# Gate and up of a ternary FFN as seven block products of half depth per four chunks and two batches, on one Trainium2 core

## What is computed

```
x = x + tanh(g_xattn) * xattn(layernorm(x), ctx, ctx, Wq, Wk, Wv, Wo, bo, g)
x = x + tanh(g_ffn)   * ffn(layernorm(x), w_gate, w_up, w_down)

def bitlinear(x, w):                       # w: 2752 x 1024, w_down: 1024 x 2752
    scale = mean(abs(w))
    q = round(clip(w / (scale + EPS), -1, 1))
    return x @ (q * scale).T
ffn(h) = bitlinear(bitlinear(h, w_gate) * bitlinear(h, w_up), w_down)
```

## Time and profile before

| | |
|---|---|
| median of 3 runs | 1417.92 us (1417.47 to 1419.09) |
| the profiled execution's own time | 1416.91 us |
| its span, first to last instruction | 1415.1 us |
| TensorE's mean granted clock | 0.985 |
| matmuls, each with a weight load | 9528 |

### The profile page before, as it was taken

The page is one execution under the profiler, slowest core; times in us unless marked ns, Lnnn a source line. Parts: engine busy times, 40 slices in busy tenths (PEclk is TensorE's granted clock), DMA queues, the critical chain, the costliest instruction groups (busy, mean ns, idle before and its releaser), DMA issues.

```text
span 1415.1 us, 23736 instructions
## 1 busy us (share of the span) xinstructions
PE 1350.5 (95%) x9528; PEld 959.8 (68%) x9528; DVE 903.9 (64%) x1369; ACT 623.3 (44%) x957; POOL 452.4 (32%) x275
## 2 busy tenths in 40 slices
PE   4786799999999999999999999999999999999999
PEld 2464487756787468774788558785787658875884
DVE  6968788877787557675675667775675747521220
ACT  4768887653545234533444333542344334320220
POOL 0159816845332413333332133323322222110000
PEclk7998999999999999999999999999999999999999
DMA  9939999976535733556433553446633644121001
GB/s 357 408 141 306 288 283 299 266 153 164 127 60 105 164 90 61 105 107 148 104 75 76 127 142 76 100 85 144 134 76 61 130 101 98 31 52 54 2 1 45
DMA packets 328429, 189.04 MB, mean 134 GB/s; under 512 B 295872, under 2 KB 296000, under 8 KB 328320
## 3 DMA queue, kind: packets, MB, share of 16 engines
q1 hardware_dynamic: 321408, 162.37, 46.7%
q10 hardware_dynamic: 6912, 25.17, 5.5%
HBM read 97.32 MB, written 16.78 MB: 81 GB/s over the span
## 4 chain that ended last, share of the span: by engine, by line
PE 82%; DVE 5%; issue 4%; DMA 3%; POOL 3%; ACT 1%; SPq 1%; ACTq 0%; POOLq 0%; DVEq 0%
PE ps L905 37%; PE ps L930 21%; PE ps L693 6%; PE ps L695 6%; PE ps L694 6%; PE ps L873 2%; DMA w_dn<-in_gate_w 1%; DMA stage_c<-in_down_tail 1%; PE ps L881 1%; PE ps L790 1%; POOL qs L1525 1%; DVE inter_buf L1150 1%; PE ps L861 1%; DVE absum L1203 1%; POOL w_dn L1495 1%
## 5 line engine op out<-in xcount | busy, mean ns | idle before, releaser
L905 PE MATMUL ps<-zT,w_gu 128*128 128x256 f16 x5504 | 626.2, 273 | 0.8 <-DVE gate L1450 0.7
L905 PEld LDWEIGHTS ps<-zT,w_gu 128*128 128x128 fp8e4 x5504 | 538.9, 98 | 81.3 <-DVE gate L1450 1.3
L930 PE MATMUL ps<-w_dn,inter_buf 128*128 128x512 fp8e4 x1376 | 304.4, 379 | 5.0 <-DVE inter_buf L1150 2.5
L930 PEld LDWEIGHTS ps<-w_dn,inter_buf 128*128 128x128 f16 x1376 | 134.6, 99 | 161.2 <-issue 6.0
L1525 POOL TENSOR_TENSOR qs<-qs,q_stat 128x1024 f32<-128x1024 f32 x64 | 126.8, 1984 | 296.6 <-DVE q_stat L1393 296.5
L942 ACT ACTIVATE gate<-ps 128x256 f32<-128x256 f32 (+1 forms) x176 | 67.1, 381 | 271.3 <-PE ps L905 268.3
L1450 DVE SCALAR_TENSOR_TENSOR gate<-ps,gate 128x256 f32<-128x256 f32 (+1 forms) x176 | 73.1, 416 | 109.2 <-ACT gate L942 108.3
L1531 POOL TENSOR_TENSOR rsv<-ssv,cst 128x4 f32<-128x4 f32 x32 | 36.7, 1147 | 240.2 <-DVE ssv L1404 240.2
L1292 DVE TENSOR_REDUCE kmx<-ps 128x1 f32<-128x1024 f32 x64 | 78.0, 1218 | 52.5 <-PE ps L695 48.9
L942 ACT ACTIVATE inter_buf<-gate 128x256 f16<-128x256 f32 (+1 forms) x176 | 72.5, 412 | 86.6 <-DVE gate L1450 86.6
L1046 ACT ACTIVATE ek<-ps,kbias,k_unit 128x1024 f32<-128x1024 f32 x56 | 67.3, 1202 | 92.8 <-DVE kbias L1301 92.8
(11 more groups left out here) (174 smaller groups left out, 1939.6 us busy)
## 6 DMA issues: line engine op xcount, KB each, us to landing
w_dn<-in_down_w SPq DMA_DIRECT2D x19, 512.0 KB, 7.0
xb<-in_x ACTq DMA_DIRECT2D x16, 512.0 KB, 4.8
x_dram<-xb SPq DMA_DIRECT2D x16, 512.0 KB, 2.9
fin<-x_dram SPq DMA_DIRECT2D x32, 256.0 KB, 3.0
out<-fin SPq DMA_DIRECT2D x32, 256.0 KB, 2.1
inter_buf<-in_up_w SPq DMA_DIRECT2D x15, 512.0 KB, 10.6
inter_buf<-in_gate_w SPq DMA_DIRECT2D x14, 512.0 KB, 9.4
w_dn<-in_gate_w SPq DMA_DIRECT2D x14, 512.0 KB, 9.2
```

The costliest lines, as they stand in the source:

```text
L905: last = nc.tensor.matmul(ps[:, j % 2, s * T:s * T + T], w_gu[:, w, k, :], zT[:, h, k, :], start=(k == 0 and h == 0), stop=(k == NC - 1 an ...
L930: mm = nc.tensor.matmul(ps[:, hf, :], lhs, w_dn[:, j, hf * 512:hf * 512 + 512], start=(u == 0), stop=(u == total - 1))
```

## The change

For groups 1 to 7, gate and up of the chunks 0 to 19 are computed in five blocks (`SU`) of four chunks. The depth of 1024 is halved (low, high), the four chunks are two pairs (half 0, half 1) and the two batches are the columns' halves. Instead of eight products of a half depth, a pair and a batch, seven are made from sums: of the weights (values -2 to 2 in fp8) and of z of the two batches. Each product (`product(g, s, q)`) is 4 weight columns x 4 depth blocks x 2 f16 halves = 32 matmuls of 128 columns in one PSUM bank. Chunk 20 and the tail keep the old way (`gu`), as does group 0.

- **Weight forms.** 35 forms (5 blocks x 7) of 128 x 2048 bytes go to a DRAM tensor `forms` in two DMAs each (`store_form`, on SP's queue) while group 0 runs. Three of seven are the quantized weights themselves; four are sums: q = 4 and q = 1 on VectorE, q = 2 and q = 5 on GpSimd, mostly in place in `w_gu` (q = 1 waits until group 0 has used the block's chunks). The first load waits for all 35.
- **Ring.** `load_form` (SP) brings a form back for each of the 245 products, 256 KB each, into a ring of 8 places; a load waits for the product 8 before it. The ring and the buffers `z16`, `zF`, `blocks` lie in the space of `w_gu` that is free by then.
- **z.** `z` moves from GpSimd to VectorE for batches 2 to 15 and works in place in `xb`, after `st_x2` has landed. When both batches' halves are made, GpSimd forms four half-width sums of z in place (`z_sum`), which are split (`zs_hi` on ScalarE, `zs_lo` on VectorE) and transposed (`turn_zs`) into `zF`. `ld_xr` of the next batch waits for this.
- **Evictions.** Products alternate between the two banks. Of seven, ScalarE copies three out (slots 0, 1, 6), VectorE adds four onto earlier ones (slots 2 to 5). Then `pair_mul` on GpSimd multiplies gate and up, `pair_hi` on ScalarE and `pair_lo` on VectorE split the result, two of each per block of 4 chunks.
- **Order.** `WHEN` is new as a whole: 3717 steps. In it 39 of the 44 `wsign` steps of gate and up stand before the first `gu` (33 before the change).

The core of the diff (the constants, the helpers of addresses and the lists of positions are left out):

```diff
-Z_SCALE = 2.0 ** 10
-I_SCALE = 2.0 ** -5
+Z_SCALE = 2.0 ** 8
+I_SCALE = 2.0 ** -6
+B_SCALE = 2.0 ** -3 / Z_SCALE
+SU = 5
+SLOTS = 7 * SU
+RING = 8
+ACT_SLOTS, DVE_SLOTS = (0, 1, 6), (2, 3, 4, 5)
+        def slot_bank(g, s, q):
+            return (first_bank(g) + 7 * s + q) % 2
...
+            def store_form(s, q):
+                if q in BASE_SLOTS:
+                    sp.wait_ge(wq_done, 2 * (4 * s + 4))
+                else:
+                    sp.wait_ge(form_made[q], s + 1)
+                wait(sp, form_stored[q], 32 * s)
+                rows = forms[(7 * s + q) * P:(7 * s + q + 1) * P, :]
+                for u in range(2):
+                    sp.dma_start(rows[:, u * 1024:u * 1024 + 1024].rearrange("p (m n) -> p m n", m=2),
+                                 form_place(s, q)[:, u, :, :]).then_inc(form_stored[q], 16)
+            def load_form(g, s, q):
+                n = SLOTS * (g - 1) + 7 * s + q
+                if n == 0:
+                    for f in range(7):
+                        sp.wait_ge(form_stored[f], 32 * SU)
+                    sp.wait_ge(gu_ready, J)
+                wait(sp, product_done, n - RING + 1)
+                x = 7 * s + q
+                sp.dma_start(ring[n % RING], forms[x * P:x * P + P, :]).then_inc(form_in[n % RING], 16)
...
+            def product(g, s, q):
+                n, m = SLOTS * (g - 1) + 7 * s + q, su_of(g, s)
+                pe.wait_ge(form_in[n % RING], 16 * (n // RING + 1))
+                if s == 0 and q in (1, 2):
+                    wait(pe, zF_in[q - 1], 16 * g)
+                if s == 0 and q < 2:
+                    wait(pe, inter32, gu_count(g, IC if q == 0 else IC - 1))
+                elif q < 2:
+                    if q == 0:
+                        wait(pe, evict_dve, 4 * m)
+                    else:
+                        wait(pe, evict_act, 3 * m)
+                elif q < 4:
+                    wait(pe, evict_act, 3 * m + q - 1)
+                else:
+                    wait(pe, evict_dve, 4 * m + q - 3)
+                form = ring[n % RING].rearrange("p (u m k i) -> p (u m) k i", u=2, m=2, k=4)
+                fresh = q not in (2, 4, 6)
+                for c in range(4):
+                    o = ps[:, slot_bank(g, s, q), c * P:c * P + P]
+                    for k in range(4):
+                        for h in range(2):
+                            last = nc.tensor.matmul(o, form[:, c, k, :], moving(q, h, k),
+                                                    start=(fresh and c == 0 and k == 0 and h == 0),
+                                                    stop=(k == 3 and h == 1), skip_group_check=True)
+                last.then_inc(product_done, 1)
...
 @@ block.scalar: ld_xr, evict @@
-                    wait(act, zT_in[i % GB], 16 * ((i - BY_PE) // GB))
+                    wait(act, zs_lo_s, 2 * (i // GB - 2) + 2 - i % 2)
+                    wait(act, z_summed, 4 * (i // GB - 1))
+            def evict(g, s, q):
+                if q not in ACT_SLOTS:
+                    return
+                wait(act, product_done, SLOTS * (g - 1) + 7 * s + q + 1)
+                wait(act, pair_lo_s, 2 * su_of(g, s) - 2 + (q == 6))
+                out = block_pair(g, s, q == 6)[:, 0 if q == 0 else 1, :]
+                copy(out, ps[:, slot_bank(g, s, q), :], B_SCALE).then_inc(evict_act, 1)
...
@@ block.vector: form, evict, pair_lo @@
+            def form(s, q):
+                if q == 4:
+                    dve.wait_ge(wq_done, 2 * (4 * s + 4))
...
+                elif q == 1:
+                    dve.wait_ge(form_made[4], s + 1)
+                    dve.wait_ge(gu_ready, 4 * s + 4)
+                    nc.vector.tensor_tensor(form_place(s, 1), form_base(s, 1, 0), form_base(s, 1, 1),
+                                            ALU.add, saturate=False).then_inc(form_made[1], 1)
+            def evict(g, s, q):
+                if q not in DVE_SLOTS:
+                    return
+                m = su_of(g, s)
+                wait(dve, product_done, SLOTS * (g - 1) + 7 * s + q + 1)
...
+                nc.vector.scalar_tensor_tensor(out=out, in0=ps[:, slot_bank(g, s, q), :], scalar=B_SCALE, in1=add,
+                                               op0=ALU.mult, op1=ALU.add).then_inc(evict_dve, 1)
+            def pair_lo(g, s, r):
+                wait(dve, pair_hi_s, 2 * su_of(g, s) + r + 1)
...
+                minus(out[1], v[:, :, 0, :], out[0]).then_inc(pair_lo_s, 1)
...
@@ block.gpsimd: form, pair_mul @@
+            def form(s, q):
+                if q == 2:
+                    pool.wait_ge(form_made[1], s + 1)
+                    pool.wait_ge(form_stored[0], 32 * (s + 1))
...
+            def pair_mul(g, s, r):
+                m = su_of(g, s)
+                wait(pool, evict_dve, 4 * m + (3 if r == 0 else 4))
+                if r:
+                    wait(pool, evict_act, 3 * m + 3)
+                v = block_pair(g, s, r).rearrange("p b (u m t) -> p (b u) m t", u=2, m=2)
+                nc.gpsimd.tensor_tensor(v[:, :, 0, :], v[:, :, 0, :], v[:, :, 1, :], ALU.mult).then_inc(pair_muled, 1)
```

More of the change, by code:

```diff
@@ L72 @@
 }
+FORM_ORDER = [(s, q) for s in range(SU) for q in BASE_SLOTS + SUM_SLOTS]
 SLOT = [0, 1, 2, 3, 4, 5, 6, 7, 8, 9, 10, 11, 12, 0, 1, 2, 3, 4, 5, 6, 7, 8, 9, 10, 11, 12, 0, 1, 2, 3, 4, 5, 6,
@@ L341, in every_step @@
           for kind, (each, first, end) in BATCH_STEPS.items()}
-    of["gu"] = [(g, n // 2, n % 2) for g in range(G) for n in range(2 * J - 1)]
+    of["gu"] = [(0, n // 2, n % 2) for n in range(2 * J - 1)]
+    of["gu"] += [(g, j, s) for g in range(1, G) for j, s in ((IC, 0), (IC - 1, 0), (IC - 1, 1))]
     of["down"] = [(g, n // DOWN_PARTS, n % DOWN_PARTS) for g in range(G) for n in range(4 * DOWN_PARTS)]
     for kind in ("gcopy", "gmul", "i_hi", "i_lo"):
-        of[kind] = [(g, j) for g in range(G) for j in range(J)]
+        of[kind] = [(0, j) for j in range(J)] + [(g, j) for g in range(1, G) for j in (IC, IC - 1)]
+    of["store_form"] = FORM_ORDER
+    of["form"] = [(s, q) for s in range(SU) for q in SUM_SLOTS]
+    of["load_form"] = of["product"] = of["evict"] = [(g, x // 7, x % 7) for g in range(1, G) for x in range(SLOTS)]
+    for kind in ("pair_mul", "pair_hi", "pair_lo"):
+        of[kind] = [(g, s, r) for g in range(1, G) for s in range(SU) for r in range(2)]
+    of["z_sum"] = [(g, n) for g in range(1, G) for n in range(4)]
+    for kind in ("zs_hi", "zs_lo", "turn_zs"):
+        of[kind] = [(g, a) for g in range(1, G) for a in (1, 0)]
     for kind in ("reload", "finish", "st_out"):
@@ L420, in gated_attention_ffn @@
         ct_raw = sb("ct_raw", [P, N])
+        sums = ct_raw[:, :].bitcast(F8).rearrange("p (r n) -> p r n", r=2)
+        ring = [spare[:, 28672 + r * 2048:28672 + r * 2048 + 2048] if r < RING_LOW else sums[:, r - RING_LOW, :]
+                for r in range(RING)]
         q_raw, qn16 = sb("q_raw", [P, N]), sb("qn16", [P, 2, N], F16)
@@ L1116, in z_hi @@
             def z_hi(i, _):
+                g = i // GB
                 wait(act, z_ready, i + 1)
-                wait(act, x2_stored, 16 * (i + 1))
-                copy(halves(xb[:, i % 2, :])[:, 0, :], z32).then_inc(z_hi_s, 1)
+                wait(act, zF_in[i % 2], 16 * (g - 1))
+                if g == 1:
+                    for q in range(7):
+                        act.wait_ge(form_stored[q], 32)
+                    act.wait_ge(gu_ready, 4)
+                copy(z16[i % 2][:, 0, :], xb[:, i % 2, :]).then_inc(z_hi_s, 1)
@@ L1130, in i_hi @@
             def i_hi(g, j):
-                wait(act, inter32, g * J + j + 1)
-                if j == 0:
+                wait(act, inter32, gu_count(g, j))
+                if g and j == IC:
                     wait(act, down_ready, 4 * g)
```

471 lines of the change are left out of this document (307 added, 164 removed), and 205 rows, old and new, of the table WHEN.

## The result

The changed kernel takes 1412.33 us (median of 20 runs, 1409.43 to 1421.26); the kernel before, run beside it, 1419.59 (20 runs, 1416.57 to 1433.55). The ratio is 0.993, with a 95% interval of 0.9907 to 0.9954: faster by 7 us by the medians, where 28 were forecast. Ratios here compare the means of the executions of the usual, faster state, so they can differ a little from the ratio of two medians. The profiled execution took 1418.48, span 1416.7, 6 us over its median, while the profiled 1416.9 of before is 2.7 under the 1419.59. So stages compared between these two profiles show the change 9 us slower than the medians do.

The account below looks back on a forecast made before the run. TensorE was taken as the bound, dense after 167 us. Span 1415.1 - 50.9 (matmuls) + 16 (head) + 3 (group 1) + 4 (groups 2 to 5) = 1387.2, with 1.8 around it 1389 us; range 1376 to 1403, chance 0.50.

Parts of the forecast that it names:

- The head and group 0: Up to group 1: added sums, stores and reordered steps cost +16 us, bounds 0 and +26.
- The sums: Group 0: eight VectorE sums of about 2.5 us add 20 us; at 83% busy the stage needs 137 us (+24).
- The stores: Group 0: storing 28 forms, 7.3 MB, means 26 us of transfers if DMA binds.
- The z sums' transposes: End of each group: the z-sum chain ends some 25 us after the last residual, covered by down's 37 us.
- the pace: Products: load and 128-column matmul pairs run 55.9 ns apart, 32 in about 1.95 us with the last record.
- rival (d): Products: pairs at 98 ns make the kernel slower, 1719 us; chance 0.05.
- matmul term of 50.9 us: Groups 1 to 7: 489.2 us of gate and up matmuls go, 438.3 of products come, gain 50.9 us.
- +1 per group for late evictions: Groups 2 to 5: late evictions cost +1 us each; group 1 has +3, groups 6 and 7 have 0.
- rival (c): Groups 1 to 5: late VectorE evictions hold PE at the bank, 50 us instead of 7, 1432 us; chance 0.13.
- The ring: Form loads for products: 256 KB lands in 3.0 us, ring is 14 us deep, cost 0.
- rival (b): Whole kernel: faster but most given back, head +26, evictions +12, 1403 to 1415 us; chance 0.14.
- Rival (a): Head: it takes the forms up for nothing, 1366 to 1376 us; chance 0.14.

Follow-up runs that it names:

- run 14: Changed kernel without sums, one form stored, late in group 0, shared steps in the old order up to group 1's first gate and up: 1376.12 us, ratio 0.9670.
- run 9: Changed kernel without sums, only the first form stored and read by every ring load, new order kept: 1387.26 us, ratio 0.9749.
- run 4: Changed kernel with GpSimd's and VectorE's sums cut to 128 of 2048 elements and nearly all stores to 64 of 1024 bytes a partition: 1389.08 us, ratio 0.9766.
- run 5: Changed kernel with all sums and stores short, shared steps in the old order up to group 1's first gate and up: 1398.12 us, ratio 0.9830.
- run 6: Changed kernel whole, shared steps in the old order up to group 1's first gate and up: 1419.63 us, ratio 0.9991.
- run 11: Kernel before with only the changed kernel's order of the shared steps up to group 1's first gate and up: 1439.60 us, ratio 1.0132.
- run 1: Changed kernel with GpSimd's two sums per block over 128 of 2048 elements a partition: 1395.44 us, ratio 0.9820.
- runs 12: Changed kernel whole, with VectorE's seven sums of absolute values of the down weights made on ScalarE: 1422.43 us, ratio 0.9986.
- 13: Changed kernel whole, with VectorE's down-weight sums on ScalarE and GpSimd's sums cut into four pieces: 1418.32 us, ratio 0.9970.
- 16: Changed kernel whole in the old order, sums 50 steps later in the list and stores at least 25 behind their sums: 1430.52 us, ratio 1.0059.
- runs 3: Changed kernel with all but the first two form stores writing 64 of 1024 bytes a partition: 1410.70 us, ratio 0.9919.
- run 7: Changed kernel whole, with GpSimd's sums cut into four instructions of 512 elements each: 1411.66 us, ratio 0.9933.
- run 56: Not a follow-up run: in "matmul run 56 ns apart" the word run is a verb and 56 ns is the spacing; no kernel, time or ratio belongs to it.

## Why the prediction failed

The step that failed is "The head and group 0", its +16 us within bounds of 0 and +26. It is +46.1 in the profile, with +30.5 from the first gate and up to the first down alone, over the 30 at which the prediction calls itself wrong. Taken apart, by the starts of gu(1):

| step | gu(1) | us |
|---|---|---|
| before | 341.9 | |
| z sums and the rest of the change (run 14) | 344.7 | +2.8 |
| the new order (run 9) | 359.1 | +14.4 |
| the short steps of the forms by being there (run 4) | 362.1 | +3.0 |
| sums and stores in full length (changed kernel) | 388.0 | +25.9 |

The shares hold for this sequence alone. By way of the old order the same 46.1 are +2.8 (run 14), +22.6 for the short steps (run 5), +21.7 for their length (run 6) and -1.0 for the new order. Either way the full length of sums and stores is over 20 us, and the stores are under one of them; how much goes to the order and how much to the short steps isn't one number.

- **The order**, 14.4 here and 18 us by run 11, had no term. The prediction named the 39 steps against 33 and gave them no price, though each is 1.1 us of ScalarE put ahead of the first gate and up, with three more `wquant` of 1.2 us on GpSimd (44 and not 41). That these are what makes gu(0) 11 us later is not shown: the runs exchanged the whole order. TensorE goes into the first gate and up without a gap in both kernels, out of attention matmuls; its last wait ahead of it is for VectorE's zT and ends at 164.6 before and at 172.9 after.
- **The sums.** I priced them by VectorE's share: 20 us of work, 114 into 137 us at 83%. The sums' time was right (2.66 us each against 2.5), and the stage of 112.6 us came to 141.2, near the 137. But that was the sum of other things: VectorE stood 13.4 us longer in i_lo and 2.9 in p (7 x (2046 - 1625) ns), because GpSimd's sums of 4.1 to 4.3 us (I had 3.3) exclude it; short sums give 16.1 and 3.3 of that back (run 1). The rows of before showed it: i_lo's mean of 509 ns over all groups is 718 in group 0 against 413 alone. I used the mean. The Trainium skill's rule on the shared port pair (page "SBUF — State Buffer", section "Who interferes with whom") says the same; an estimate by it, eight GpSimd sums of 4.2 us that each exclude VectorE, adds up to 34 us to the upper bound.
- **The stores** at up to 26 us in the bounds cost 0.9.
- **Half clock.** No term had it. About 19 of the 46 us are TensorE at 1.2 GHz; the forecast took each stall at its own length.
- **The z sums' transposes** were put at nothing, covered by down. In the changed kernel's profile TensorE waits 2.1 us for them at the start of group 1, more in runs 12, 13 and 16.

What was right: the pace. Products' matmuls are 56 ns apart: 32 of them last 1.95 us with the last record, and the next block of 32 starts 1.79 us behind, as in group 7 of the changed kernel:

```profile
1313.53 1.95 PE L1064 MATMUL ps<-zT,w_gu 128*128 128x128 f16 x32
1315.32 2.90 PE L1064 MATMUL ps<-w_gu 128*128 128x128 f16 x49
```

So rival (d) is out. The 81 ns of the Trainium skill (page "TensorE: Matmul & The Clock Gate", section "Back-to-back issue gap") are out with it: the trace disagrees with that sentence. The matmul term of 50.9 us held: from the start of group 2 to the end before took 1415.1 - 512.8 = 902.3 us, after 1416.7 - 557.3 = 859.4. That is 42.9 less, where six sevenths of 50.9 are 43.6; the +1 per group for late evictions was not needed. Group 1 got 1.6 of its 7.3 back (170.9 to 169.3 us). In runs 3 and 7, which are the changed kernel in this part, it takes 162.2 at a clock of 1.00 (run 7's period):

```profile
386.80:549.10 162.30, 160.61 (x1686) 118.19 (x1685) 133.74 (x175) 74.71 (x98) 72.66 (x41) 1.00 0.82 192
```

So 7 us of the changed kernel's profiled execution are a wait for the z sums, another of 3.3 us behind it and a stretch at half clock, about what that execution lies over its median of 1412.3; without them group 1 gets back 8.7, more than its 7.3. TensorE waits 0.9 us in all for an eviction from group 1 on, so rival (c) is out; its eviction is cheaper than thought (684 ns against 748, x140) and 0.8 us of slack was enough. The ring holds: a load lands after 3.1 us, and no wait of TensorE for it shows. The longest wait in front of a product is the 2.1 us for the transposed z sums:

```profile
PE ps L1064 <- issue: 2.1, 1, 2.1
PE ps L1064 <- DVE w_gu L1695: 0.9, 2, 0.5
```

In sum: the forecast's span was 1387.2; head +30.1 over it, group 1 +2.7, the rest -3.3, which is 1416.7. The outcome is rival (b), "most given back", by its head and not by its evictions: it had +26 and +12, the runs show +46 and next to nothing, so that its 1403 to 1415 holds the result is in part luck. Rival (a) was no fantasy: without sums and in the old order the kernel takes 1376.1 (run 14), at the upper end of its 1366 to 1376.

## What to carry to other kernels

Before pricing work that is added to VectorE or GpSimd, split the rows of its neighbours by what the other engine does: an instruction with two SBUF operands that takes 413 ns alone and 906 beside GpSimd says that each long GpSimd instruction will be paid on VectorE too. A busy share doesn't say what a microsecond is worth: taking 8.4 us off VectorE gave nothing, taking 20 off another place 17. And an order written anew is a change of its own: run it alone on the old kernel first, as run 11 did, where it cost 18 us. That doesn't mean that the old order saves them in the new kernel: with the forms in, it gave nothing (run 6). Last, a profiled execution can lie 6 us off its median; look in the profiles of its neighbours for the stretch that does it.

## What the runs showed of the hardware

- VectorE's i_lo, with two SBUF operands, mostly waits out a GpSimd instruction that is under way and ends 0.27 to 0.29 us after it (10 of the 13 that met one so in group 0 of the changed kernel): 413 ns becomes up to 4052 beside a GpSimd sum of 4.0 us. With the sums in pieces of 1.4 us the longest is 2118, beside qs. One operand in PSUM: 411 and 413 ns, no difference.
- GpSimd seems to be held in turn: a qs, 1.9 us at the least, lasts 3.88 where a VectorE sum started 0.16 us ahead of it.

```profile
238.71 2.28 DVE L1672 TENSOR_TENSOR w_gu<-w_gu 128x2048 fp8e4<-128x2048 fp8e4 x1
238.87 3.88 POOL L1784 TENSOR_TENSOR qs<-qs,q_stat 128x1024 f32<-128x1024 f32 x1
```

- 8-bit operands bring VectorE next to nothing in a sum of two: 2048 elements take 2.28 us alone, 1.11 ns an element, against 1.19 with 1024 elements of 32 and 16 bits (1.22 us). GpSimd takes 4.1 to 4.3 us for the same sum, in four pieces 5.6.
- Pairs of weight load and 128-column matmul run 56 ns apart, one load each, over 7840 of them.
- TensorE's granted clock fell to 1.2 GHz in or behind six of the nine pauses of 1.8 to 4.6 us that it made between 207 and 339 us. From gu(0) to gu(1) half clock cost about 10 us beside some 26 more of idle time.
